# Expert prologue: gates with stationary weights, choice by batch, ranks by two products and a scan, weights landed in place

## What is computed

```python
x = hidden_states.reshape(-1, H)
logits = x @ gate_w.T + gate_b
top_vals, top_idx = jax.lax.top_k(logits, TOP_K)
routing = jax.nn.softmax(top_vals.astype(jnp.float32), axis=-1).astype(x.dtype)
for e in range(E):
    h = x @ w1[e].T + b1[e]
    x_glu = h[:, 0::2]
    x_lin = h[:, 1::2]
    y = x_glu * jax.nn.sigmoid(1.702 * x_glu) * (x_lin + 1.0)
    ye = y @ w2[e].T + b2[e]
    we = jnp.sum(routing * (top_idx == e), axis=-1)
    out = out + ye * we[:, None]
```

## Time and profile before

| | |
|---|---|
| median of 3 runs | 1338.8 us (1334.45 to 1339.3) |
| the profiled execution, its own time | 1323.27 us |
| its span, first to last instruction | 1321.5 us |
| busy in the span | PE 1080.6, PEld 894.1, DVE 723.4, ACT 457.8, POOL 504.1 us |
| mean granted TensorE clock | 0.879 of full speed |
| stage 0 prologue | 0 to 89.07 us |
| stage 1 prologue | 569.6 to 651.49 us |

### The profile page before, as it was taken

The page is one execution under the profiler, slowest core; times in us unless marked ns, Lnnn a source line. Parts: engine busy times, 40 slices in busy tenths (PEclk is TensorE's granted clock), DMA queues, the critical chain, the costliest instruction groups (busy, mean ns, idle before and its releaser), DMA issues. The chain is left out here.

```text
span 1321.5 us, 18371 instructions
## 1 busy us (share of the span) xinstructions
PE 1080.6 (82%) x6352; PEld 894.1 (68%) x6352; DVE 723.4 (55%) x1715; ACT 457.8 (35%) x796; POOL 504.1 (38%) x526
## 2 busy tenths in 40 slices
PE   5459995259999999545599993999969999879997
PEld 5447884246566666345488883888858888768886
DVE  7334432557777776163454435565444667745564
ACT  3203332126666766122043320233223334213222
POOL 7425663245363522055255640000116789600000
PEclk9999998567999999755599996999975898879999
DMA  6312223200000000153133224000020030000001
GB/s 218 103 44 84 89 88 111 78 0 1 1 2 17 1 17 17 49 174 114 32 118 123 93 74 134 1 1 1 0 76 0 1 64 1 0 1 14 7 14 32
DMA packets 36447, 66.05 MB, mean 50 GB/s; under 512 B 6116, under 2 KB 27653, under 8 KB 35975
## 3 DMA queue, kind: packets, MB, share of 16 engines
q1 hardware_dynamic: 28678, 43.90, 11.0%
q0 software_dynamic: 7680, 20.98, 4.9%
HBM read 43.89 MB, written 20.97 MB: 49 GB/s over the span
## 5 line engine op out<-in xcount | busy, mean ns | idle before, releaser
L1575 PE MATMUL ps<-had_xt,w 128*128 128x512 f32 x768 | 194.4, 404 | 4.7 <-DVE had_xt L136 4.7
L1575 PEld LDWEIGHTS ps<-had_xt,w 128*128 128x128 f32 x768 | 143.4, 193 | 36.1 <-DVE had_xt L136 5.5
L1401 DVE CUSTOM_DVE_ANT_0 ps<-ps,att_mask 128x128 f32<-128x128 f32 (+3 forms) x256 | 119.1, 516 | 43.1 <-PE ps L1053 42.9
L530 PE MATMUL ps<-moe_w,moe_narrow_xb 128*128 x480 | 129.1, 405 | 0.0
L445 POOL DMA_INDIRECT moe_xs<-xn_rows,moe_index x80 | 78.8, 985 | 96.3 <-DVE moe_index L751 54.2
L451 POOL DMA_INDIRECT made_rows<-moe_units_made,moe_index x80 | 80.0, 1000 | 82.5 <-ACT moe_units_made L622 70.3
L1639 DVE TENSOR_TENSOR had_gated<-ps,had_sig 128x512 f32<-128x512 f32 x64 | 44.3, 692 | 122.4 <-ACT had_sig L1610 122.4
L530 PEld LDWEIGHTS ps<-moe_w,moe_narrow_xb 128*128 128x128 f32 x480 | 93.3, 195 | 20.5
L1610 ACT ACTIVATE had_sig<-ps 128x512 f32<-128x512 f32 x64 | 38.2, 597 | 189.5 <-PE ps L1575 189.5
L771 DVE TENSOR_TENSOR moe_narrow_xb<-ps,moe_narrow_xb 128x512 fp32r<-128x512 f32 x40 | 27.7, 692 | 137.9 <-ACT moe_narrow_xb L604 137.9
L1280 ACT ACTIVATE att_early_probs<-ps 128x384 f32<-128x384 f32 (+1 forms) x192 | 90.8, 526 | 29.8 <-PE ps L1068 28.5
(11 more groups left out here) (240 smaller groups left out, 2393.1 us busy)
## 6 DMA issues: line engine op xcount, KB each, us to landing
moe_units_raw<-in_moe SPq DMA_DIRECT2D x16, 770.0 KB, 5.2
moe_w<-made_rows SPq DMA_DIRECT2D x16, 512.0 KB, 4.9
xn_rows<-moe_wide_xn SPq DMA_DIRECT2D x8, 512.0 KB, 6.3
x<-x_turned SPq DMA_DIRECT2D x8, 512.0 KB, 7.8
x<-in_x SPq DMA_DIRECT2D x4, 512.0 KB, 5.4
x_turned<-x SPq DMA_DIRECT2D x4, 512.0 KB, 2.9
moe_narrow_later<-in_w SPq DMA_DIRECT2D x4, 512.0 KB
x_turned<-x SPq DMA_DIRECT2D x1, 2048.0 KB, 6.7
```

What stands on the lines that cost most here:

```text
L530: last = nc.tensor.matmul(h_bank(j, i), xb[a][:, j % 2, i, k, :], weight(c), start=False, stop=(k == KC - 1 and c == 1))
L1401: last = nc.vector.tensor_tensor_reduce(g.ps[:, a, col:col + n], g.ps[:, a, col:col + n], mask[:, SEQ - n:SEQ], -1.0, 3.0e38, ALU.add, ALU ...
L1575: last = nc.tensor.matmul(g.ps[:, bank(n, half), :], w[a][:, k, c * P:(c + 1) * P], xt[low][:, b % 2, k, :], start=(k == 0 and q == 0), st ...
```

## The change

The change is inside `experts_stage`, so it acts in both stages.

- **Gates.** The gate weights become the stationary operand and 512 tokens the moving one: 4 products a batch (L468 to L473 after) in place of 24. High and low gate columns stand side by side (16 rows out). ScalarE copies the 16x512 result out (`across`), and 4 small products with `both` (L482) turn it and add its halves.
- **Choice by batch.** VectorE adds the bias and takes the maxima of a batch (`choose`) as its logits come, between its normalisations.
- **Ranks.** 32 products become 2 (L506, L507); VectorE makes the sums over earlier tiles with one scan of 128 elements, and some more small operations follow it.
- **Token numbers.** `slot_row` is written in two halves, and TensorE starts its 16 products of the first half when that is there.
- **Weights land in place.** The records go straight to `w[1]`, with no wait for a buffer; the biases of all experts come by one transfer of their own (`b1_all`, 1024 pieces of 16 bytes). ScalarE writes the high half to `w[0]`, and VectorE subtracts in place (`low_weights`), in place of POOL.
- The bias rows are made earlier, and the halving of the routing weights is moved behind the loop.

```diff
-        gate_r = [sb(f"gate_r{q}", [P, KC, E], F32R) for q in range(2)]
+        gate_r = sb("gate_r", [P, KC, 2, E], F32R)
+        both = sb("both", [2 * E, E])
+        across = sb("across", [2 * E, 2, SEQ])
+        b1_all = sb("b1_all", [P, E, 2 * IC])
...
 
+            sp.dma_start(b1_all[:, :, :], ins["moe"].rearrange("e p n -> p e n")[:, :, REC_W1 + REC_W2:REC]) \
+                .then_inc(b1_here, 16)
+
             def record(e):
-                if e >= 2:
-                    sp.wait_ge(hi_split, e - 1)
-                    sp.wait_ge(lo_split, e - 1)
-                sp.dma_start(raw[:, e % 2, :], ins["moe"][e]).then_inc(rec_here[e % 2], 16)
-            record(0)
-            record(1)
+                sp.dma_start(f32(w[1][:, e, :]), ins["moe"][e][:, 0:REC_W1 + REC_W2]).then_inc(rec_here[e], 16)
+            for e in range(E // 2):
+                record(e)
             for b in range(BATCH):
                 sp.wait_ge(norm.xn_done, b + 1)
                 sp.dma_start(by_tiles(g.xn_dram[:, :], b), g.xn[:, b, :, :]).then_inc(xn_stored, 16)
-                for e in (2 * b + 2, 2 * b + 3):
...
-                b1 = raw[:, s, REC_W1 + REC_W2:REC]
-                nc.gpsimd.tensor_copy(b1_src[:, :, e], b1)
-                nc.gpsimd.tensor_copy(b1_src[:, :, LO_ROW + e], b1)
-                pool.wait_ge(hi_split, e + 1)
...
-                low(2 * b)
-                low(2 * b + 1)
+                norm.rstd(pool, b)
+            pool.wait_ge(b1_here, 16)
+            for r in (0, LO_ROW):
+                last = nc.gpsimd.tensor_copy(b1_src[:, :, r:r + E], b1_all[:, :, :].rearrange("p e q -> p q e"))
...
             def gates(b):
                 pe.wait_ge(norm.lo_done, b + 1)
-                steps = [(a, c, k) for k in range(KC) for a, c in ((0, 0), (0, 1), (1, 0))]
+                if b >= 2:
+                    pe.wait_ge(gates_out, b - 1)
+                bank = g.ps[:, 2 + b % 2, :]
+                nc.tensor.matmul(bank[0:2 * E, :], gate_r[:, 0, :, :].rearrange("p a e -> p (a e)"),
+                                 xt[0][:, b % 2, 0, :], start=True, stop=False, skip_group_check=True)
+                for k in range(KC):
+                    nc.tensor.matmul(bank[0:E, :], gate_r[:, k, 0, :], xt[1][:, b % 2, k, :],
+                                     start=False, stop=False, skip_group_check=True)
+                nc.tensor.matmul(bank[0:2 * E, :], gate_r[:, 1, :, :].rearrange("p a e -> p (a e)"),
+                                 xt[0][:, b % 2, 1, :], start=False, stop=True, skip_group_check=True) \
+                    .then_inc(gates_ps, 1)
+
...
+                pe.wait_ge(gates_out, b + 1)
+                if b >= 2:
+                    pe.wait_ge(logits_added, b - 1)
                 for i in range(BT):
-                    t = b * BT + i
-                    for q, (a, c, k) in enumerate(steps):
-                        last = nc.tensor.matmul(g.ps[:, 0, t * E:(t + 1) * E], xt[a][:, b % 2, k, i * P:(i + 1) * P],
...
                 last.then_inc(logits_ready, 1)
-            for b in range(BATCH):
-                norm.turn(pe, b, 4 + 2 * (b % 2))
-                if b:
-                    gates(b - 1)
...
+            norm.turn(pe, 1, 6)
+            gates(0)
+            norm.turn(pe, 2, 4)
+            gates(1)
+            pe.wait_ge(both_done, 1)
+            logits_of(0)
+            norm.turn(pe, 3, 6)
+            gates(2)
+            logits_of(1)
+            gates(3)
+            logits_of(2)
+            pe.wait_ge(b1_filled, 1)
             for q in range(2 * IC):
                 last = nc.tensor.transpose(Y_BANK[:, q * P:(q + 1) * P], b1_src[:, q, :], g.ident[:, :])
             last.then_inc(b1_turned, 1)
+            logits_of(3)
+
+            pe.wait_ge(chosen_done, 1)
+            by_expert = chosen[:, :, :].rearrange("p t e -> p e t")
+            nc.tensor.matmul(g.ps[:, 2, 0:TILES * E], g.ones[:, :], by_expert, start=True, stop=True)
+            nc.tensor.matmul(g.ps[:, 3, 0:TILES * E], g.strict[:, :], by_expert, start=True, stop=True) \
+                .then_inc(ranked, 1)
+            for r in range(2):
+                pe.wait_ge(spread, r + 1)
+                for n in range(r * TILES, (r + 1) * TILES):
+                    last = nc.tensor.matmul(g.ps[:, 1, 0:NB], slot_row[:, n, :], slot_token[:, n, :],
+                                            start=(n == 0), stop=(n == 2 * TILES - 1))
+            last.then_inc(tokens_ps, 1)
...
             def high(e):
-                act.wait_ge(rec_here[e % 2], 16 * (e // 2 + 1))
...
-            for b in range(BATCH):
+                act.wait_ge(rec_here[e], 16)
+                nc.scalar.activation(w[0][:, e, :], f32(w[1][:, e, :]), ACT.Copy).then_inc(hi_split, 1)
+
+            def high_norm(b):
+                if b >= 2:
+                    act.wait_ge(gates_ps, b - 1)
+                norm.high(act, b, 4 + 2 * (b % 2), xt[0][:, b % 2, :, :])
+
+            def out_of_gates(b):
+                act.wait_ge(gates_ps, b + 1)
                 if b >= 2:
                     act.wait_ge(logits_ready, b - 1)
-                norm.high(act, b, 4 + 2 * (b % 2), xt[0][:, b % 2, :, :])
-                high(2 * b)
...
-            nc.scalar.activation(route[:, 1, :], margin[:, :], ACT.Sigmoid).then_inc(route_done, 1)
+                nc.scalar.activation(across[:, b % 2, :], g.ps[0:2 * E, 2 + b % 2, :], ACT.Copy).then_inc(gates_out, 1)
+            high_norm(0)
+            high_norm(1)
+            out_of_gates(0)
+            high(0)
+            high_norm(2)
+            out_of_gates(1)
+            high(1)
+            high_norm(3)
+            out_of_gates(2)
+            high(2)
+            out_of_gates(3)
...
+            for e in range(3, E):
+                high(e)
+            act.wait_ge(margin_done, 1)
+            nc.scalar.activation(route[:, 0, :], margin[:, :], ACT.Sigmoid, scale=-1.0).then_inc(route_done, 1)
...
+            def low_weights(e):
+                dve.wait_ge(hi_split, e + 1)
+                nc.vector.tensor_tensor(w[1][:, e, :], f32(w[1][:, e, :]), f32(w[0][:, e, :]), ALU.subtract) \
+                    .then_inc(lo_split, 1)
...
+            def choose(b):
+                mine = slice(b * BT, (b + 1) * BT)
+                dve.wait_ge(logits_ready, b + 1)
+                nc.vector.tensor_tensor(logits[:, mine, :],
+                                        g.ps[:, b % 2, 0:BT * E].rearrange("p (t e) -> p t e", e=E),
+                                        gate_b[:, :].unsqueeze(1).to_broadcast([P, BT, E]), ALU.add) \
+                    .then_inc(logits_added, 1)
+                dve.wait_ge(logits_added, b + 1)
+                for t in range(b * BT, (b + 1) * BT):
+                    last = nc.vector.max(top[:, t, :], logits[:, t, :])
+                last.then_inc(top_done, 1)
...
+                if b >= 2:
+                    choose(b - 2)
...
+            choose(2)
+            low_weights(0)
+            low_weights(1)
+            choose(3)
+            nc.vector.tensor_tensor(margin[:, :], top[:, :, 1], top[:, :, 0], ALU.subtract).then_inc(margin_done, 1)
...
+            dve.wait_ge(b_hi, 2)
+            nc.vector.scalar_tensor_tensor(out=b1_row[:, :], in0=f32(b1_hi[:, :]), scalar=g.minus_low[:, :],
+                                           in1=Y_BANK, op0=ALU.mult, op1=ALU.add).then_inc(b_row, 1)
...
+            nc.vector.tensor_tensor_scan(flat_of(total), f32(g.ones[:, 0:TILES * E]), in_tile, 0.0,
+                                         ALU.mult, ALU.add).then_inc(routed, 1)
+            nc.vector.tensor_reduce(padded, in_tile.rearrange("p (e t) -> p e t", e=E), AX_X, ALU.add) \
+                .then_inc(routed, 1)
...
+            for r in range(2):
+                mine = slice(r * TILES, (r + 1) * TILES)
+                nc.vector.tensor_tensor(slot_row[:, mine, :], g.column[:, :].unsqueeze(1).to_broadcast([P, TILES, P]),
+                                        pos[:, 2, mine].unsqueeze(2).to_broadcast([P, TILES, P]), ALU.is_equal) \
+                    .then_inc(spread, 1)
+            for e in range(2, 4):
+                low_weights(e)
...
+            for e in range(4, E):
+                low_weights(e)
...
+            dve.wait_ge(route_done, 2)
+            nc.vector.tensor_scalar(route[:, :, :], route[:, :, :], 0.5, None, ALU.mult).then_inc(combined, 1)
...
```

158 lines of the change are left out of this document (67 added, 91 removed).

## The result

| | before | after |
|---|---|---|
| median, and the runs | 1337.55 us (1334.45 to 1339.3, 4 runs) | 1304.36 us (1298.72 to 1305.88, 4 runs) |
| ratio, 95% interval | | 0.9759 (0.9725 to 0.9794) |
| the profiled execution, span | 1323.27, 1321.5 us | 1303.65, 1301.9 us |
| prologue of stage 0, of stage 1 | 84.0, 81.9 us | 68.8, 65.5 us |
| expert loop of stage 0, of stage 1 | 117.9, 121.6 us | 127.1, 129.2 us |

By the ratio the kernel is 32.2 us faster (27.5 to 36.8); the medians differ by 33.2. A prologue is measured here from the stage's first statistics (L91) to its first expert product (L525, now L538), the loop from there to the start of the last such product (the two expectations on the loop count 1.4 us more, to the last product of L530 or L543). The prologues gained 15.2 and 16.4 us, 31.6 together.

A forecast was written before the change was run, and what follows sets the result against it. Prologues were taken as bound by one chain of small steps through all engines. Gains of 15.35 us (stage 1) and 15.85 (stage 0), together 31.2, off the median 1338.8 gave 1307.5 us, range 1291 to 1321.

The forecast's parts named there:

- A: Prologue up to `chosen`: unstretched normalisations, new gates and choices by batch bring `chosen` to 607.8 from 618.32, gain 10.5 us.
- B: Ranks, from `chosen` to the first rank operation: two products replace 32, 7.1 becomes 1.25 us, gain 5.85.
- C: Small chain after the ranks, 5.5 us before: seven added operations less the one replaced, loss 1.6 us.
- D: Token numbers: 11.5 us becomes half of `slot_row` (2.2) plus all products (7.0), gain 2.2 us.
- E: Tail to the loop: index 1.2, owners 1.5, four low halves 7.1, tokens' low half 0.8; loss 1.6, stage 0 1.1.
- the rival that put them down to transfers: Last two normalisations of a stage: transfers, not GpSimd, stretch them, some 8 us a stage show; 1323 us, chance 0.05.
- turn 1.97, gates 2.05, logits 1.0: Steps in us for one batch on the path to `chosen`; logits taken as four small products plus a wait.
- the rival of the higher clock: Prologues: denser gates raise TensorE's clock, 20 us of work a path shrink 43%, 17 in all; 1290 us, chance 0.07.
- the rival against that: Gates: the four products don't overlap, 1.15 us more a batch, 8.7 in all with copies and waits; 1316 us, chance 0.10.
- The rival of starved gathers: Tail: second gather waits for the last low half, loop starts 4.8 us later, 9.6 in all; 1317 us, chance 0.09.
- Transfers: Loads of x, weights and biases and the stores in the prologues: predicted cost zero.
- The slower rival: Expert loop starts and stays at the lower clock, 3.6 us more a pair; 1380 us with half low, chance 0.03.

The follow-up runs named there:

- two_lows_beside: Changed kernel with the low halves of weights 0 and 1 on GpSimd, beside the fourth normalisation; 1306.20 us, ratio 0.9801 to the kernel before.
- old_gates: Changed kernel with the earlier 24 gate products a batch put back, choices still by batch; 1300.98 us, ratio 0.9739 to the kernel before.
- gaps_full: Changed kernel with low halves of weights moved into VectorE's waits and bias turns behind the last logits; 1296.79 us, ratio 0.9735 to the kernel before.
- before_again: The kernel before, profiled a second time with nothing edited; 1314.17 us in one run.
- old_ranks: Changed kernel with the earlier 32 rank products issued again ahead of the two new ones, results unused; 1294.82 us, ratio 0.9833 to the kernel before.

## Why the prediction was right

It said 1307.5 (1291 to 1321) and faster at 0.95; the median is 1304.4. The total of the prologues was forecast at 31.2 and measured at 31.6 in the first pair of profiles and 31.7 in the second. Its terms did less well than their sum, so that the sum hit within half a us is in part luck: A gave more than forecast and E took more. In stage 1:

| term | forecast | measured | from |
|---|---|---|---|
| A, up to `chosen` | +10.5 | +12.33 | 48.7 us after the first statistics before, 36.4 after |
| B, ranks | +5.85 | +6.11 | 7.10 from `chosen` to the first rank operation became 0.99 |
| C, small chain | -1.6 | -1.27 | 5.5 became 6.8 |
| D, token numbers | +2.2 | +2.13 | 11.5 became 9.4 |
| E, tail | -1.6 | -2.96 | 9.03 became 11.99 |
| sum | 15.35 | 16.34 | |

In stage 0 the first pair of profiles gave 10.0 for A (forecast 10.5), 7.0 for B to D together (6.45) and -1.8 for E (-1.1), in all 15.2 (15.85). There the higher clock came only with the gates of batch 2, and the small tables were half a us later.

**A** was right that the stretched normalisations were GpSimd's doing, shown by `two_lows_beside`, which refutes the rival that put them down to transfers, and that they would go. (The conversion's hold-up was not put back; in the kernel before it ended at 617.47 and GpSimd's subtraction beside it at 617.44.) The Trainium skill, "SBUF — State Buffer", section "Summary: rules for kernel authors", says that when VectorE is in its 2-port mode, or has two SBUF inputs while GpSimd reads SBUF, the second to issue blocks until the first has finished. The instruction of 3.50 us, which has one tensor as input and ended 0.15 behind the subtraction that had started 0.12 ahead of it, agrees with that; which mode it ran in, the trace doesn't say.

But the hold-up is not all that A took away, and the prediction's reading of before missed the rest. Ahead of the last gates what ended last was ScalarE's wait for weight records, 7.7 us from the turn to the high half, and in stage 0 7.9. The third and later records waited for a buffer to be read, and they stood ahead of the last batch on ScalarE. The prediction weighs the records only as a cost of the new kernel, at zero. Its sum didn't suffer, since it added up the new chain step by step from 580.88 and took the old one whole. In stage 1 the last gates start 10.2 us earlier, counted from the first statistics, than before; how that splits between the hold-up, the records and the clock is open, since no run put the buffers back.

What A said of the steps of the new chain was wrong. The step "turn 1.97, gates 2.05, logits 1.0" took the logits as four small products; the row shows eight, and 1.87 us, at the low clock. With copy and hand-overs a batch costs an estimated 4.7 where the step has 3.05 and 0.1. What covered the error was, first, the clock, to which the prediction gave no term. Beside the first wide products it is 0.50, and from 573.2 to 580.1 it is 1.00, that is 2.4 GHz: the turn took 1.10 instead of 1.97, the four gate products of batch 1 1.11 (574.86 to 575.97) instead of 2.05, together 1.8 us on the path, and the small products 1.05. The first choice came 1.4 earlier than forecast. Second, the last batch's logits were ready (593.04) before VectorE's two low halves ended (594.84), so their length did not show. In `old_gates` TensorE's work was unbroken, the clock in stage 1 stayed at 0.50 and every turn took 1.97, and it came out level with the change. So the rival of the higher clock was partly true, but for the work of a few us, not for the 20 us of it that the rival assumed. (That rival's end, 1307.5 less 17, also lies half a us below the stated range, though the prediction says that only the last two are outside it.) The four products did overlap (2.06), so the rival against that is refuted.

**B, C and D** were right, and B and D were confirmed by undoing them; C was only measured.

**E** named the right end in stage 1, the low halves, which ended 8.2 us after the index was there (615.48 to 623.66) where the step had 8.6. What failed is the step "low half of the tokens 0.8" behind them. It took the two arms to meet at VectorE's last subtraction. But TensorE waits for all low halves ahead of the first turn (L527 <- `moe_w`), so turn, high half, low half and hand-overs follow in a row, 2.5 us. That was in the code of before too; there the low halves were done long before, so the wait never showed. In stage 0 the same wait ended last, where the prediction had the gathers: 1.8 lost instead of 1.1. The gathers' hold-up was as feared in kind (1.79, 1.36 and 1.36, where `gaps_full` has 0.95) and cost nothing, since the gathers were not last. The rival of starved gathers is refuted by the same rows: the second got through 4.0 us after the index was there, not 8.6. (Its "6.2 later" is 6.4 by its own rows; the 4.8 that it takes into the sum stands.)

**Transfers** cost almost nothing after the change, as forecast: in its prologues ScalarE never waits for a record, and VectorE never for the stores ahead of `slot_row`. The one price is in stage 0, where VectorE's wait for the small tables (L718) is 0.98 us where it was 0.49 (0.61 to 1.07 in the other profiles with the new loads, 0.53 in `before_again`). What the prediction overlooked is that these transfers did cost in the kernel before: there ScalarE waited for records for 22.0 us in stage 0 and 21.6 in stage 1, six times each.

**The slower rival** did not come: in stage 1 the granted clock is 1.00 from 631.3, 5 us after the loop's first product, and in before it was 5.6 us.

**The base.** The prediction subtracted from the median of runs, not from the profiled time, though it had no reason for the 15.5 us between them; that this was right it could not know. The difference of two profiles, 19.6, would have misled by 12 us.

## What to carry to other kernels

When work moves to another engine and now ends last, look at what stands behind the wait for it on every engine, not only at what it feeds: a wait that was always met long before costs nothing in the old profile and sets the end in the new one. The same holds the other way round: an engine that works in the order of its program and waits for a side job (here ScalarE for weight records) holds up whatever stands behind it in that program. Cheap independent work belongs in the waits in front of the chain, not between its links; here that, one moved wait and the high products first took another 12.5 us off. Compare stages of the trace, not spans of single profiles, when the rest of a kernel can move by 16 us without an edit.

## What the runs showed that was not expected

- The kernel before took 1314.8 us on one chip and 1332 to 1336 on another. Between profiles of the changed kernel from both groups the operations in the loop are of the same length, and the difference shows as ScalarE's "remote" waits.
- In stage 1 the granted clock rose to 1.00 amid the prologue, 2.2 us after the start of the first four products with 512 columns moving (571.00 to 573.2); in stage 0 of the same profile two whole batches of such products ran at the lower level (0.78 us for the first of each, where it is 0.40 at the higher). It stayed at 0.50 through 10.38 us of unbroken products with 8 columns moving (`old_gates`) and 7.0 us of rank products (`old_ranks`).
- The four small logits products, with operands that are plain float32, show as eight instructions and take 1.87 us at the low clock for 8 columns each, nearly as long as the four wide products (2.06) for 512.
